# Local attention: mask matmuls on two 64x128 tiles instead of eight 64x32 tiles, and the waits of the value matmuls moved ahead of the mask

## The reference

```
qkv = x @ Wqkv                       # 128 -> 3 x 1024
q, k = l2norm(q) * qs, l2norm(k) * ks, then rotary with scale
# each window of 32 queries sees its own 32 keys and the 32 before it
mask = (it < jb) | (it > jb + w) | (jb == -1)
sim = einsum('bhwie,bhwje->bhwij', bq, bk2) * 8
attn = softmax(where(mask, -max, sim), -1)
out = einsum('bhwij,bhwje->bhwie', attn, bv2)
x = out.reshape(b, n, 1024) @ Wo + x
```

## Time and profile before

| | |
|---|---|
| median of 3 runs | 3997.31 us (3993.72 to 3998.38) |
| the profiled execution | 3998.38 us, of which the span of the core is 3996.6 us |
| mean granted clock of TensorE | 0.971 of 2.4 GHz |
| PE busy | 3694.6 us, 92% of the span, 71214 matmuls |
| PEld busy | 2981.2 us, 75% |
| DVE busy | 3246.0 us, 81% |
| ACT busy | 2950.7 us, 74% |
| POOL busy | 2236.4 us, 56% |
| mask matmuls L667 | 3072, mean 280 ns |
| score matmuls L674 | 24576, mean 223 ns |
| PV matmuls L686 | 24576, mean 225 ns |

### The profile page before, as it was taken

How to read it: one execution, slowest core, us unless ns; L and a number is a source line. 1 busy time by engine, 2 the same in 40 slices (tenths; PEclk the granted TensorE clock), 3 DMA queues, 4 the chain that set the end, 5 groups by cost and what they waited for, 6 DMA issues and landing times. The chain is left out here.

```text
span 3996.6 us, 190730 instructions
## 1 busy us (share of the span) xinstructions
PE 3694.6 (92%) x71214; PEld 2981.2 (75%) x71214; DVE 3246.0 (81%) x9894; ACT 2950.7 (74%) x8653; POOL 2236.4 (56%) x2298
## 2 busy tenths in 40 slices
PE   6769999989999899998999989999999998699997
PEld 4547888678887688876888768888688885477775
DVE  5878888778887788877888878888788886588886
ACT  4647888578886688866888757888578884488885
POOL 3537777467774677756777556777477771300003
PEclk8879999999999999999999999999999999799998
DMA  1013333233332233332333323333233331100000
GB/s 40 6 38 80 79 79 80 62 80 79 79 78 75 68 81 78 80 82 56 82 79 78 91 53 75 79 78 80 64 79 79 80 81 26 35 0 0 0 0 27
DMA packets 305312, 246.41 MB, mean 62 GB/s; under 512 B 74485, under 2 KB 299860, under 8 KB 304340
## 3 DMA queue, kind: packets, MB, share of 16 engines
q1 hardware_dynamic: 305108, 243.72, 24.2%
HBM read 24.54 MB, written 2.12 MB: 7 GB/s over the span
## 5 line engine op out<-in xcount | busy, mean ns | idle before, releaser
L810 ACT ACTIVATE wa_pb<-wa_sc,wa_nm 128x64 f32<-128x64 f32 x3072 | 672.4, 330 | 367.5 <-DVE wa_nm L1006 360.8
L1156 POOL TENSOR_TENSOR wa_t<-wa_t,wa_rn 128x512 f32<-128x512 f32 x768 | 786.2, 1045 | 274.6 <-DVE wa_rn L984 269.2
L1162 POOL TENSOR_TENSOR wa_t<-wa_t 128x512 f32<-128x512 f32 x384 | 497.1, 1294 | 475.2 <-DVE wa_t L960 475.1
L958 DVE TENSOR_TENSOR wa_t<-wa_pj,wa_ctab 128x512 f32<-128x512 f32 x768 | 527.3, 687 | 236.9 <-PE wa_ta L572 218.5
L44 PE MATMUL wa_pj<-lw_wqkv_high,wa_xhigh 128*128 128x512 f32 x1152 | 533.4, 463 | 77.0 <-issue 40.6
L793 ACT ACTIVATE wa_sq<-wa_pj 128x512 f32<-128x512 f32 x768 | 471.9, 616 | 114.9 <-PE wa_pj L46 112.7
L1171 POOL TENSOR_TENSOR wa_t<-wa_t 128x512 f32<-128x512 f32 x384 | 491.8, 1281 | 0.0
L46 PE MATMUL wa_pj<-lw_wqkv_high,wa_xlow 128*128 128x512 f32 x1152 | 460.0, 399 | 0.0
L45 PE MATMUL wa_pj<-lw_wqkv_low,wa_xhigh 128*128 128x512 f32 x1152 | 457.1, 397 | 0.0
L966 DVE TENSOR_REDUCE wa_raw<-wa_sq 128x16 f32<-128x1024 f32 x384 | 449.3, 1170 | 0.0
L640 PE MATMUL wa_ob<-wa_oT,wa_wo 128*128 128x128 f32 x3072 | 407.1, 275 | 0.7
(11 more groups left out here) (283 smaller groups left out, 8840.2 us busy)
## 6 DMA issues: line engine op xcount, KB each, us to landing
wa_vv<-wa_vt SPq DMA_DIRECT2D x2304, 65.0 KB
wa_vv<-wa_vt SPq DMA_DIRECT2D x1152, 32.5 KB
lw_wqkv<-L_ffn_Wqkv SPq DMA_DIRECT2D x6, 1536.0 KB
lw_xs<-yT SPq DMA_DIRECT2D x96, 64.0 KB
lw_fs<-yT SPq DMA_DIRECT2D x48, 128.0 KB
lw_xs<-yT SPq DMA_DIRECT2D x96, 63.8 KB
lw_fs<-yT SPq DMA_DIRECT2D x96, 63.8 KB
wa_wo<-L_ffn_Wo SPq DMA_DIRECT2D x6, 512.0 KB, 4.2
```

Of the source, the lines that this page charges most:

```text
L810: last = nc.scalar.activation(pb[:, u.par(2), p, e, :], SC[:, e, p * KEYS:(p + 1) * KEYS], ACT.Exp, bias=nm[:, u.par(2), e, p:p + 1])
L958: nc.vector.tensor_tensor(t1[:, b, j], x, table(ctab, slice(0, HD)), ALU.mult)
L1156: nc.gpsimd.tensor_tensor(here, here, rn[:, u.par(1), j * HG:(j + 1) * HG].unsqueeze(2).broadcast_to((128, HG, HD)), ALU.mult).then_inc(s. ...
L1162: nc.gpsimd.tensor_tensor(t1[:, b, 0], t1[:, b, 0], t2[:, b, 0], ALU.add).then_inc(s.qadd_done, 1)
```

## The change

The two `sem_inc` on `session`, and the semaphore itself, are gone. The mask is put in by two matmuls, one for each half of the rows, with 128 output columns each, in place of eight with 32. The waits of PV are asked for before the mask matmuls of the same slot; in a slot that has no scores, before the transposes of the normalised output.

```diff
@@ -653,6 +653,8 @@
                         else:
                             pe.wait_ge(s.oT_out, u.count(1, 5, 1))
+                            if u.has(3):
+                                value_waits()
                         transposes(TA, lambda p: on[:, u.par(4), p].rearrange("q e d -> q (e d)")).then_inc(s.oT_done, 1)
                     if u.has(0):
                         values(u)
@@ -660,12 +662,12 @@
                         t, h2 = u.tile(2), u.half(2)
                         pe.wait_ge(s.qk_out, u.count(2, 2, 2))
-                        pe.sem_inc(s.session, 1)
-                        for n in range(WPT):
-                            for e in range(2):
-                                r, q = tiles64(n, e)
-                                nc.tensor.matmul(SC[q, e, 0:PR * KEYS], pick[r, t, q], maskb[r, :, :], start=True, stop=False,
-                                                 skip_group_check=True)
+                        if u.has(3):
+                            value_waits()
+                        for e in range(2):
+                            half = slice(64 * e, 64 * e + 64)
+                            nc.tensor.matmul(SC[:, e, 0:PR * KEYS], pick[half, t, :], maskb[half, :, :], start=True, stop=False,
+                                             skip_group_check=True)
                         for p in range(PR):
@@ -677,8 +679,6 @@
                         last.then_inc(s.score_done, 1)
                     if u.has(3):
-                        value_waits()
-                        pe.sem_inc(s.session, 1)
                         for p in range(PR):
```

More of the change, by code:

```diff
@@ L421 @@
     "kadd_done", "v_out", "v_ready0", "v_ready1", "v_ready2", "v_ready3", "split_done",
-    "xs_ready", "proj_done", "session", "sq_done", "ss_done", "sum_done", "rn_done", "rot_done",
+    "xs_ready", "proj_done", "sq_done", "ss_done", "sum_done", "rn_done", "rot_done",
     "ln_done", "guess_done", "newton", "qadd_done", "q_ready", "k_ready", "qk_done", "qk_out", "score_done",
```

## The result

The changed kernel takes 4023.91 us (median of 5 runs, 4016.82 to 4024.67), the kernel before beside it 3998.38: 1.0057 times as long, 95% interval 1.0043 to 1.0073 (the two medians alone give 1.0064). The forecast was 3965, 0.8% less than the kernel before; the measured time lies above the range. The profiled execution took 4016.73 us with a span of 4014.9, 18.3 more than the span of before.

What follows compares the result with a forecast made beforehand. PE's own sequence was taken to bound the loop. From 3998.4 us, 36 saved (330 slots at 0.11) and 4 lost at the layers' ends gave 3966, or 3965 for the median; range 3925 to 4000.

Steps and rivals of the forecast that it cites:

- What bounds the kernel, and the hole: Local layers' loop: PE's sequence sets the time; moving PV's waits closes the pause after the scores, 0.17 us a slot.
- rival (b): Loop: the weights' copy, now ahead of mask and scores, makes PE wait and halves the gain, 3983 us; chance 0.10.
- (d): Between scores and PV: pause stays, 4021 us (0.10 shared with rival (c)), or half stays and effects cancel, 3998 (0.10).
- the sum: Steady-state slots: 0.17 gained less 0.06 lost saves 0.11 us a slot, 36 us over 330 slots.
- The mask's own delay: Mask to first score in each slot: 0.13 us later, 0.09 for the shape change and 0.04 for the weight load.
- half slope: Mask's weight load: bf16 columns cost half the f32 time per column, so 96 more add 0.04 us.
- How much of it reaches the end of the block: Score block: of the mask's 0.13 us delay, 0.07 is won back, so the scores end 0.06 later (0 to 0.18).
- the stock of 64 instructions: Instructions ready at block start: with two masks instead of eight, six more scores start fast, giving 0.07 us back.
- PV behind the scores: PV directly after the scores: between 0.08 us lost and 0.11 gained, rounded to nothing.
- The starts: Layer starts, where PE's code first comes from memory: some 40 slots counted with no gain.
- The ends of the layers: Layer ends without V projection: three waits of 0.45 us a layer, 8 us in six layers, half taken: 4 (0 to 8).
- Rival (c): Every slot: tile change and slower PV outweigh the removed pause, 0.09 us longer, 4031 us; 0.10 shared with (d)'s bad half.

Runs made afterwards that it cites:

- the version: Kernel before with PV's waits moved ahead of the mask except at the layers' ends, old mask kept: 0.9978 of before; with 64 added increments 0.9970, with 128 0.9997.

## Why the prediction was wrong

- *What bounds the kernel, and the hole.* Right. PE's sequence sets the time; the hole of 0.18 went when the waits did, and no wait for ACT or DVE came up in the loop, so rival (b) did not happen and (d) is out. (In the sum, the way into 64x32 is 0.33 - 0.22 = 0.11, which I wrote as 0.10; nothing hangs on it.)
- *The mask's own delay.* Forecast 0.13 (0.09 for the change of shape, 0.04 for the load), measured 0.09. The shape's share was right, to a hundredth. The load costs nothing that shows: 92 ns against 89, and my half slope did not hold. The Trainium skill (TensorE: Matmul & The Clock Gate, Weight-path perf modes) says that the fast weight load is on with 128 weights and an input that is not FP32, and gives about twice the speed as measured on trn2. 92 ns against 192 for 128 f32 columns agrees, though those loads differ in rows too.
- *How much of it reaches the end of the block.* This step failed. I let six more scores come out of the stock of 64 instructions and took 0.06. The last score comes 0.11 later, and a slot costs 0.14 with the mask alone, 0.09 on top of moved waits. Of the scores 24 start in the first 0.19 us as before, and the next nine take 0.10 us (33 in the first 0.29), which is the slow pace of 11 ns: the six that I let come out of a bigger stock did not come sooner.
- *PV behind the scores.* I rounded it to nothing. With the waits alone PV's last part is 0.15 longer in two of four slots, so the waits bring 0.10 a slot in place of 0.17. This step failed too. Together a turn gains 0.05 us (3.7 over 72 turns) where the sum said 0.44: the loop's 36 us became 4.
- *The starts.* I gave them no gain and no cost. With the old mask the joined block costs 14 to 22 us there, a little under half of it as more idle time and the rest with PE busy, the clock being at 1.2 GHz for 37 to 46 us. The prediction did not price the clock at all. With the new mask the stops and the low clock (18.9 us) are nearly as before, and the changed kernel comes out at -2. That this agrees with my nothing is luck.
- *The ends of the layers.* Forecast 4 (0 to 8), measured 23. This step failed, and it decided the sign. By themselves the moved waits cost 11 in the ends of the trace, 13 in the timed runs; in the changed kernel undoing them gave 14 and 21. I priced ACT's copy, halved it for idle time that was there, and took the third slot for the same case. But there `value_waits` also asks for DVE's addition of the output projection of the same slot, and PE waits 0.84 for it. The rest are longer stops of PV and, in four of the six ends, the clock at 1.2 GHz for 13.7 us; at half speed that is some 7 us, my estimate. With the new mask the ends are 8 to 12 us above before even where no wait moved in them; the place of the code can do as much, and which of the two it is stays open.

So the sign was decided by the ends: -6 in the loop and the starts, +23 behind them. Rival (c) had the sign right and the place of the loss wrong: it put the loss into every slot, and there mask and PV together stayed just below the hole.

## What to carry to other kernels

A wait moved ahead of other work must be priced in every form that the code takes, the drained ends of a pipeline first: there the work that covered it is missing, and here six ends outweighed 72 turns. In a block of small tiles keep one shape from the first matmul to the last; four times fewer instructions did not pay for one more change of shape. And where code runs for the first time, for differences of a few tenths of a percent compare the places of the profile, not two totals: increments that do nothing moved this kernel by 0.35%, the change by 0.57%. And compare the granted clock place by place: a stop costs more than its own length if TensorE is slower behind it.

## What the runs showed of the hardware

A change from 64x128 or from 64x64 tiles to 64x32 tiles costs 0.09 to 0.11 us, as from the whole array (0.11). That these drain the array is the Trainium skill's reading (TensorEngine Tiling (Array Packing), Key Properties); the price is from the rows above. A weight load of 128 bf16 columns took 92 ns, one of 128 f32 columns 192. Increments of a semaphore ahead of PE's program cost little for 64 of them (0.4 us or, against the version's own lead of -1.4, 1.8), and 4 to 5 us for 128. A stop in newly run code got longer, 2.35 in place of 1.30 us, when the code ahead of it ran faster. And behind two stops, of 1.73 and 2.35 us, the granted clock was 0.50 (1.2 GHz), behind the one of 1.30 it was 1.00; in the starts of the layers the time at 1.2 GHz went from 14.7 to 46.4 us when only the waits of PV had moved.
